# Second quantised product in pairs of batches with its rounding on ScalarE, and a last norm taken batch by batch

## The reference, cut to what matters

```
def _smooth_quant_linear(x, w):
    s  = sqrt(max|x| over rows / max|w| over rows)      # one per channel
    xs, ws = x / s, w * s
    x_scale, w_scale = max|xs| / 127, max|ws| / 127     # one per row
    return round(xs / x_scale) @ round(ws / w_scale).T * x_scale * w_scale.T

h = _smooth_quant_linear(x[b], fside[b]);  gate, up = split(h)
y = _smooth_quant_linear(silu(gate) * up, ctx[b])       # the second product
x = layernorm(x + y)                                    # norm of stage 1
```

## Time and profile before

| what | value |
|---|---|
| median of 3 runs | 496.03 us (494.37 to 498.11) |
| the profiled execution, its own time | 497.61 us |
| its span from first to last instruction | 495.9 us |
| TensorE busy | 408.3 us, 82% |
| VectorE busy | 346.8 us, 70% |
| ScalarE busy | 239.2 us, 48% |
| GpSimd busy | 108.8 us, 22% |
| mean granted TensorE clock | 0.929 of full |

### The profile page before, as it was taken

The page is one execution under the profiler, slowest core; times in us unless marked ns, Lnnn a source line. Parts: engine busy times, 40 slices in busy tenths (PEclk is TensorE's granted clock), DMA queues, the critical chain, the costliest instruction groups (busy, mean ns, idle before and its releaser), DMA issues.

```text
span 495.9 us, 8112 instructions
## 1 busy us (share of the span) xinstructions
PE 408.3 (82%) x3100; PEld 313.1 (63%) x3100; DVE 346.8 (70%) x786; ACT 239.2 (48%) x440; POOL 108.8 (22%) x113
## 2 busy tenths in 40 slices
PE   3955577998887654889998689999987899999993
PEld 2525555776655442679666546667756789888883
DVE  2499797787888668676658797657835586667545
ACT  1296804655438743767568414546526234422220
POOL 4500007349421631151470000000003610001001
PEclk9987798999998685799999899999988999999997
DMA  6900020000000000000000009930000000000101
GB/s 194 306 15 1 7 66 3 3 4 1 2 1 1 1 1 0 1 0 2 1 1 1 1 2 133 110 114 3 2 1 0 1 1 1 0 1 2 42 2 42
DMA packets 13126, 13.33 MB, mean 27 GB/s; under 512 B 2904, under 2 KB 12448, under 8 KB 12832
## 3 DMA queue, kind: packets, MB, share of 16 engines
q1 hardware_dynamic: 12224, 12.54, 11.1%
q10 hardware_dynamic: 864, 0.27, 0.2%
HBM read 11.56 MB, written 1.05 MB: 25 GB/s over the span
## 4 chain that ended last, share of the span: by engine, by line
PE 60%; DVE 24%; ACT 10%; issue 3%; POOL 1%; DMA 1%; ACTq 0%; DVEq 0%; POOLq 0%
PE PS L2272 12%; PE PS L2289 6%; PE PS L1873 4%; PE PS L1957 4%; DVE mx L1309 4%; ACT arena L776 3%; PE PS L391 3%; PE PS L1998 3%; PE PS L1851 3%; PE PS L1925 3%; PE PS L1967 2%; PE PS L2213 2%; PE PS L2200 2%; DVE mx L1304 2%; DVE arena L1201 2%
## 5 line engine op out<-in xcount | busy, mean ns | idle before, releaser
L912 ACT ACTIVATE PT<-PS 128x512 f32<-128x512 f32 x96 | 53.4, 594 | 37.0 <-PE PS L1925 36.9
L2272 PE MATMUL PS<-arena_r 128*128 128x512 f32 x264 | 64.5, 393 | 1.5 <-ACT xT L776 1.5
L680 POOL TENSOR_SCALAR va<-mv 128x4 f32<-128x4 f32 x12 | 5.5, 454 | 264.7 <-DVE mv L1148 264.7
L2272 PEld LDWEIGHTS PS<-arena_r 128*128 128x128 f32 x264 | 48.1, 188 | 11.3 <-issue 2.2
L776 ACT ACTIVATE arena<-PS 96x1024 bf16<-96x1024 bf16 (+4 forms) x54 | 39.7, 785 | 17.5 <-PE PS L1851 10.5
L1851 PE MATMUL PS<-ident,arena 128*96 128x128 bf16 x416 | 30.8, 240 | 20.6 <-DVE arena L1191 17.1
L1873 PE MATMUL PS<-masks,ident 128*128 128x512 bf16 x112 | 43.0, 384 | 5.2 <-DVE mx L1309 2.8
L1851 PEld LDWEIGHTS PS<-ident,arena 128*96 128x96 bf16 x416 | 28.6, 139 | 24.7 <-issue 12.2
L1309 DVE TENSOR_REDUCE mx<-PS 128x4 f32<-128x1024 f32 x32 | 39.0, 1220 | 1.7 <-PE PS L1908 0.6
L2289 PEld LDWEIGHTS PS<-arena_r 128*128 128x128 f32 x264 | 34.4, 191 | 2.5 <-DVE arena_r L1659 0.9
L2289 PE MATMUL PS<-arena_r 128*128 128x256 f32 x264 | 35.1, 283 | 0.7 <-DVE arena_r L1659 0.7
(11 more groups left out here) (235 smaller groups left out, 917.9 us busy)
## 6 DMA issues: line engine op xcount, KB each, us to landing
arena<-in_L_ffn_w SPq DMA_DIRECT2D x16, 176.0 KB, 9.9
arena<-in_L_ffn_w SPq DMA_DIRECT2D x2, 1024.0 KB, 11.1
arena<-in_L_ffn_w SPq DMA_DIRECT2D x2, 704.0 KB, 6.3
arena<-in_fside_BxS2xS SPq DMA_DIRECT2D x1, 1024.0 KB, 12.2
out<-x SPq DMA_DIRECT2D x4, 256.0 KB, 2.2
x<-in_x SPq DMA_DIRECT2D x1, 768.0 KB, 8.6
arena<-in_L_attn_Wq SPq DMA_DIRECT2D x2, 256.0 KB, 4.4
arena<-in_L_attn_Wo SPq DMA_DIRECT2D x2, 256.0 KB, 5.8
```

What stands on the lines that cost most here:

```text
L912: nc.scalar.activation(PT[:, n % 2, 512 * j:512 * (j + 1)], bank(3 + j), ACT.Exp, scale=NEG_SCALE)\
L2272: last = mm(bank(2 * (n % 2) + gu), wp[c][:, gu, c_ * P:(c_ + 1) * P], xp[5][:, c, blk * 512:(blk + 1) * 512], start=(step == 0 and c == 0 ...
```

## The change

- Second product by pairs: the gated values are turned and copied two batches at a time, and maxima, ratios, roots and scaled operands are formed for pair 0 and then for pair 1.
- `round2` is split: VectorE keeps the row scales (`row_scales2`), ScalarE does the four multiply-and-add instructions of 128 columns (`rounded2`).
- The queues of all engines are reordered: residuals 0 and 1 and the norm of pair 0 stand between the steps of pair 1; the context's transposes and copies are spread out (batches 0 and 1 early, 2 and 3 behind `products2(2)`) and use one bank, 5; the integer transposes use one bank, 4. GpSimd does both gated values and the roots of pair 1 ahead of `scaled_weights(2)` and `(3)`.
- ScalarE loads the table of Silu ahead of `integers(2)` by a probe of one element.
- `scaled_to_rows(2)` stands ahead of `products(0)`; VectorE's `row_scales1(2)` ahead of the context's reciprocal and maxima.
- The end: down(20) whole, then down(21) by halves; `low_part(20)` ahead of `gated(21)`; statistics, inverse deviations and application for batch 2 and batch 3 on their own.

```diff
@@ GpSimd
             gated(0)
+            gated(1)
             scaled_weights(1)
-            gated(1)
-            scaled_weights(2)
+            smooth_roots(3, 0, 2)
             gated(2)
             gated(3)
+            smooth_roots(4, 2, B)
+            scaled_weights(2)
             scaled_weights(3)
-            smooth_roots(3, 0, B)
...
-            inverse_deviations(5, 2)
+            for b in (2, 3):
+                lo = 2 * (b % 2)
+                pool.wait_ge(variances, normed(5, 2) // 2 + 1 + b % 2)
+                alone(pool.tensor_scalar(va[:, lo:lo + 2], mv[:, lo:lo + 2, 1], LN_EPS, None, ALU.add))
+                alone(pool.tensor_tensor(rstd[:, lo:lo + 2], va[:, lo:lo + 2], exponents[:, 0, 0:2], ALU.pow), rstd_ready)
@@ ScalarE
+            def rounded2(b):
+                act.wait_ge(row_scales_ready, B + b + 1)
+                if b < 2:
+                    act.wait_ge(Q["q16"], B)
+                for i in range(4):
+                    ins = nc.scalar.activation(q32[:, b % 2, i, 0:CX], bank(b, CX, i * CX), ACT.Identity,
+                                               bias=roundup[:, 0:1], scale=rrq[:, b, i:i + 1])
+                ins.then_inc(Q["q32b"], 1)
...
+            nc.scalar.activation(table_probe[:, :], ones[:, 0:1], ACT.Silu)
+            integers(2)
+            silu(0)
+            silu(1)
+            copy_row_scales(2)
+            integers(3)
+            copy_aT(0)
+            copy_row_scales(3)
+            copy_qT(2)
+            copy_qT(3)
+            silu(2)
+            copy_attT(0)
+            silu(3)
+            copy_attT(1)
+            rounded2(0)
+            copy_aT(1)
+            integers2(0)
+            rounded2(1)
+            copy_qT2(0)
+            integers2(1)
+            copy_row_scales2(0)
+            copy_qT2(1)
+            rounded2(2)
+            copy_row_scales2(1)
+            integers2(2)
+            copy_qT2(2)
+            copy_attT(2)
+            copy_row_scales2(2)
+            copy_attT(3)
+            rounded2(3)
             evac_xT(2, 0, 1)
             integers2(3)
             evac_xT(2, 1, 2)
@@ VectorE
+            gated_maxima(0)
+            scaled_product(2)
+            smooth_scales(3, 0, 2)
+            scaled_operands2(0)
+            scaled_operands2(1)
+            scaled_product(3)
+            row_scales2(0)
+            row_scales2(1)
...
-            round2(0)
-            round2(1)
-            round2(2)
+            gated_maxima(1)
+            smooth_scales(4, 2, B)
+            scaled_operands2(2)
+            scaled_operands2(3)
             quantised_residual(0)
+            row_scales2(2)
             quantised_residual(1)
-            norm_pair(1, 0)
-            round2(3)
+            norm_stats(1, 0)
+            row_scales2(3)
+            norm_apply(1, 0)
             low_x(2, 0, 2)
             quantised_residual(2)
...
             for n in range(2 * EC):
+                if n == 2 * EC - 1:
+                    low_part(n - 1)
                 gated(n)
-                if n >= 1:
+                if 1 <= n < 2 * EC - 1:
                     low_part(n - 1)
@@ TensorE
+            scaled_to_rows(2)
+            products(0)
+            products(1)
+            scaled_to_rows(3)
+            spread_row_scales(2)
+            spread_row_scales(3)
+            gated_transposes(0)
+            quant_transposes(pe, 2)
+            quant_transposes(pe, 3)
+            products(2)
+            products(3)
+            context_transposes(0)
+            scaled_to_rows2(0)
+            scaled_to_rows2(1)
+            context_transposes(1)
+            gated_transposes(1)
             quant_transposes2(pe, 0)
+            products2(0)
+            scaled_to_rows2(2)
+            scaled_to_rows2(3)
             quant_transposes2(pe, 1)
-            products2(0)
             products2(1)
             quant_transposes2(pe, 2)
             products2(2)
+            context_transposes(2)
+            context_transposes(3)
             transpose_x(2, 0, 2)
             quant_transposes2(pe, 3)
...
+            down(2 * EC - 2)
             for tiles in (range(0, 2), range(2, 4)):
-                down(2 * EC - 2, tiles)
                 down(2 * EC - 1, tiles)
```

More of the change, by code:

```diff
@@ L997, in _, with copy_aT, copy_attT @@
             context_exponentials(3)
[L998 to L1011, removed]
-                act.wait_ge(Xs["tr"], b + 1)
-                copy(attT[:, b, :, :].rearrange("p a b -> p (a b)"), bank(4 + b % 2)).then_inc(Xs["attT"], 1)
+            def copy_aT(pair):
+                act.wait_ge(Q["atr"], pair + 1)
+                copy(aT[:, 2 * pair:2 * pair + 2, :].rearrange("p a b -> p (a b)"), bank(2 * pair)).then_inc(Q["aT"], 1)
+            def copy_attT(b):
+                act.wait_ge(Xs["tr"], b + 1)
+                copy(attT[:, b, :, :].rearrange("p a b -> p (a b)"), bank(5)).then_inc(Xs["attT"], 1)
+            def rounded2(b):
[6 more added lines that the diff above has]
+                ins.then_inc(Q["q32b"], 1)
             def integers2(b):
                 act.wait_ge(Q["q32b"], b + 1)
+                if b < 2:
+                    act.wait_ge(Q["qtr"], B)
+                else:
+                    act.wait_ge(Q["qtr2"], b - 1)
                 nc.scalar.activation(q16[:, b % 2, :, 0:CX], q32[:, b % 2, :, 0:CX], ACT.Copy, bias=-MAGIC)\
@@ L1158, in norm_apply, with batch_stats, batch_apply @@
                         ins.then_inc(x_normed, 1)
+            def batch_stats(b):
+                r = sums_of(5, b)
+                dve.wait_ge(out_read, 16 + b + 1)
+                lo = 2 * (b % 2)
+                for i in range(2):
+                    ins = v.bn_stats(stat[:, lo + i, :], r[:, b % 2, i, :])
+                link(ins)
+                for i in range(2):
+                    ins = v.bn_aggr(mv[:, lo + i, :], stat[:, lo + i, :])
+                ins.then_inc(variances, 1)
+            def batch_apply(b):
+                r = sums_of(5, b)
+                dve.wait_ge(rstd_ready, normed(5, 2) // 2 + 1 + b % 2)
+                for i in range(2):
+                    k = 2 * (b % 2) + i
+                    ins = v.tensor_scalar(x[:, 2 * b + i, :], r[:, b % 2, i, :], mv[:, k, 0:1], rstd[:, k:k + 1],
+                                          ALU.subtract, ALU.mult)
+                ins.then_inc(x_normed, 1)
             def norm_pair(stage, b):
@@ L1701, in _ @@
             outputs(1)
[L1702 removed]
+            batch_apply(2)
+            batch_apply(3)
         @block.tensor
@@ L2174, in products2 @@
                     pe.wait_ge(Q["wbc2"], b - 1)
+                else:
+                    pe.wait_ge(Q["q32b"], b + 1)
                 for k in range(2):
```

102 lines of the change are left out of this document (41 added, 61 removed).

## The result

The kernel after took 491.28 us as the median of 17 runs (487.30 to 494.77), the kernel before 496.83 in as many. The ratio is 0.9891, with a 95% interval of 0.9867 to 0.9914: about 5.4 us less (4.3 to 6.6). The forecast was 495.7 with a range down to 490.5. The time lies in the range, but the gain is over 1%, to which the prediction gave a chance of 0.13, and it comes from a stage that was forecast as a loss.

What follows compares the result with a forecast made beforehand. The prediction saw an unbroken chain of waits from about 158 us to `ffn_up`, changing hands between engines, almost only VectorE from 182 to 198. +0.5 there and -0.8 at the end took 496.03 to 495.7 us, range 490.5 to 499.0.

Steps and rivals of the forecast that it cites:

- The first product: Up to the first product's end: `integers(2)` starts at 161.6 instead of 163.1, `scaled_product(3)` ends at 173.9 instead of 173.5.
- of these 1.6 us little arrives: At the front, `integers(3)` ends near 167.0 instead of 168.6, but little of that reaches the first product's end.
- Up to the roots: From the first product's end to pair 1's roots: roots at 181.0 instead of 179.0, a loss of 2 us.
- rival 4: ScalarE's roundings cost 0.25 apart or less, so pair 0 is done before VectorE needs it: 494.7 us, chance 0.08.
- From the roots to the norm: From pair 1's roots to pair 0's variances: a gain of 2.8, eaten by 2.7 for held-up operands; variances at 192.8.
- The three kinds of rows: Trace rows cited against free operands of pair 1, read as VectorE and GpSimd taking turns by whole instructions.
- Rival 1: Pair 1's operands are not held up by GpSimd, so 2.8 us come back: 492.9 us, chance 0.22.
- From there to `ffn_up`: From `rounded2(2)` to `ffn_up`: 13.7 us, 1.7 later than before; 0.5 later at the middle clock.
- Rival 3: Low clock and ScalarE's queue together, at context(2) and (3) through one bank: slower, 499.0 us, chance 0.15.
- The end: After `low_part`: residual 0.1 earlier and last application 0.7 instead of 1.38, a gain of 0.8, bounds 0.3 and 1.3.
- The sum: Whole kernel: +0.5 up to `ffn_up` and -0.8 at the end give -0.3 on the median 496.03, so 495.7 us.
- rival 1 at a better clock: Pair 1's operands free of GpSimd and a favourable clock: 490.5 us, the range's lower end; 0.06 of rival 1's 0.22.

## Why the prediction was wrong about the stage

The forecast had `ffn_up` 0.5 us later; it came 4.05 earlier, 4.55 better. The prediction counted from 201.2, a piece of the chain; the first matmul of `ffn_up` before is at 200.86. Its forecast is 201.7, and 196.8 was measured, so its steps have to account for 4.9. In the time of before (1.1 added to the rows of after) they are these.

**The first product: starts right, worth wrong.** `integers(2)` was to start at 161.6, and it did (160.52 + 1.1). The step "of these 1.6 us little arrives" failed. `scaled_product(3)` was to end 0.4 later than before, at 173.9, and ended at 173.2, 0.3 earlier. Taken out by themselves, load and front order cost 1.3 and 1.5 of the stage, and together an estimated 1.7.

**Up to the roots: sign right, size wrong.** Forecast 2.0 later, measured 0.3 later (179.3 against 179.0). The rounding's price held: four instructions of 128 columns in 1.50, as forecast, so rival 4 fell too. The Trainium skill ("ScalarE: Activation LUTs", What ACT_TABLE_LOAD costs) has a price per column, one for each pointer and an overlap; an estimate from these figures is 1.64 for the four, near the 1.50. Of the 1.7 that the step is off, 0.7 is the front's, above. The gated values of pair 1 were turned at 174.6 and not at 175.7: they did not stand behind eight context tiles but waited for GpSimd's last gated value (173.46, idle 0.64). `aT(1)` was to be there at 178.2 and was at 176.8. GpSimd's roots of two columns took 0.73 and not 1.04, which gave the rest.

**From the roots to the norm: the step that carried the error.** The gain of 2.8 was seen, and then cancelled by 2.7 for operands of 0.92 behind a scaled weight each. Measured, the roots-to-variances stretch is 9.9 us where 11.8 was forecast and 13.9 was before. Four operands took 1.87 us, against 1.05 free and 4.0 forecast, and with the weights made to wait the stretch is 0.5 shorter. The three kinds of rows cited the earlier trace rows were two with GpSimd's tensor_tensor, and one of the large `whole_numbers` slowing GpSimd; none had a VectorE operand beside a scaled weight. The bound was taken from the row of the wrong form. Rival 1 (492.9) was nearer: the operands are held up by 0.7 of the 2.7.

**From there to `ffn_up`.** From the rounding of batch 2 it took 11.4 us; 12.5 was forecast, between 13.7 at the lower clock and 11.5 at the upper. The clock was the lower for most tiles. The surplus is the tile count: the prediction has 1.9 for a context, the price of eight tiles, but a context has four, and took 1.06 and 1.09. Rival 3's place, the two contexts through one bank, is in the chain, but moving them away gained only 0.3 to 0.4 beyond the contention. The parts add up: 1.7 up to the roots, 2.0 from the roots to batch 2's rounding, 1.1 behind it, 4.9 in all (rounded).

**The end: right.** 0.8 forecast, 0.88 measured in the profiled execution. The residual gained nothing (0.1 forecast), GpSimd 0.3, the application 0.65. The early store costs nothing.

**The sum.** With these sizes the prediction's own steps give -4.05 - 0.88 = -4.9, so 491.1 on its median of 496.03, where 491.28 was measured. That the measured time lies in the range is owed to rival 1 at a better clock, which set the lower bound; the clock was not better (0.63 against 0.67). What the prediction also missed is how the pairs and the queue order hang together. It costed the pairs as a loss of 2 us that "buys that pair 0 is rounded by then"; of this 0.3 was real, and in this order the kernel without them loses 6.2 us.

## What to carry to other kernels

Where a stage waits for a common maximum, see whether the first half's chain can run while the second half is still being made; price the split by when the first half's last consumer starts, not by the second half's delay, and reorder the queues with it: undone without its order, it costs more than it brought. Price two engines on one port by a row with both forms of instruction, or measure the pair alone: here the wrong form made 0.7 us into 2.7 and hid the gain. Where totals of the same code vary by 1%, judge an edit by the length of the stage it touches, between two landmarks that no edit moves. Then look whether the difference begins where the edit acts: here 0.45 us of two edits' results stood in the trace ahead of them.

## What the runs showed of the hardware that was not expected

- VectorE's tensor_scalar of 128x256 f32 takes 347 ns alone, 522 beside GpSimd's tensor_scalar, 751 beside its tensor_tensor. GpSimd itself loses little in the mean of eight, 922 to 939 and 722 to 773.
- GpSimd's power of two columns takes 0.73 us, of four 1.04; two columns are not half the price.
- Stretches with the same instructions differ from one profiled execution to another by more than 1%, 278.5 to 282.4 us, and TensorE's busy time in them from 258.5 to 262.1. The last exponential came anywhere from 158.3 to 164.2 us, although nothing that it waits for was changed.
- The same four matmuls of `products(2)` took 1.06 us in one trace and 0.61 in another, and what hangs on them came 0.45 us apart.
